# Weighing a head pair's values over eight query blocks instead of four, with row sums inverted once per half and the bias products opening the scores' sum

## The reference

```python
qkv = x @ w_qkv.T
qkv = qkv.reshape(b, t, dh, 3, h).transpose(3, 0, 4, 1, 2)
q, k, v = (qkv[0], qkv[1], qkv[2])
scores = jnp.einsum('bhid,bhjd->bhij', q, k) * scale
rel = jnp.arange(t)[None, :] - jnp.arange(t)[:, None] + (t - 1)
bias = rel_bias[rel]
scores = scores + bias.transpose(2, 0, 1)[None]
attn = jax.nn.softmax(scores, axis=-1)
out = jnp.einsum('bhij,bhjd->bhid', attn, v)
out = out.transpose(0, 2, 1, 3).reshape(b, t, h * dh)
return out @ w_out.T
```

## Time and profile before

| what | value |
|---|---|
| median of three runs | 2592.14 us |
| the profiled execution | 2590.8 us |
| its span, first to last instruction | 2589.0 us |
| PE busy over the span | 2448.0 us (95%) |
| DVE busy | 2157.6 us (83%) |
| ACT busy | 2032.1 us (78%) |
| POOL busy | 1519.4 us (59%) |
| PE matmuls of L1907 | 16384, 294.7 us busy |
| mean granted TensorE clock | 0.985 of full speed |

### The profile page before, as it was taken

How to read it: one execution, slowest core, us unless ns; L and a number is a source line. 1 busy time by engine, 2 the same in 40 slices (tenths; PEclk the granted TensorE clock), 3 DMA queues, 4 the chain that set the end, 5 groups by cost and what they waited for, 6 DMA issues and landing times. The chain is left out here.

```text
span 2589.0 us, 118567 instructions
## 1 busy us (share of the span) xinstructions
PE 2448.0 (95%) x52349; PEld 1956.1 (76%) x52349; DVE 2157.6 (83%) x2455; ACT 2032.1 (78%) x4077; POOL 1519.4 (59%) x1029
## 2 busy tenths in 40 slices
PE   6799999999999999999999998699999999997999
PEld 2478888888888888888888887367776777775787
DVE  5798888889888888888888886489888988895898
ACT  4689988989999898888999886667676766764776
POOL 3788888888888888887898874123222222222110
PEclk9999999999999999999999999799999999999999
DMA  3244434443444344434443332113132323221221
GB/s 96 52 98 95 109 78 96 95 110 84 99 100 98 84 93 98 96 87 97 104 99 83 85 82 60 46 43 74 40 71 49 67 47 67 50 60 28 83 74 41
DMA packets 275793, 202.01 MB, mean 78 GB/s; under 512 B 117568, under 2 KB 215880, under 8 KB 274248
## 3 DMA queue, kind: packets, MB, share of 16 engines
q1 hardware_dynamic: 275280, 194.42, 31.6%
HBM read 36.96 MB, written 1.11 MB: 15 GB/s over the span
## 5 line engine op out<-in xcount | busy, mean ns | idle before, releaser
L516 POOL TENSOR_TENSOR lt_t_sin<-lt_qk,lt_tab 128x512 f32<-128x512 f32 x384 | 685.5, 1806 | 218.9 <-DVE lt_qk L1302 216.8
L521 POOL TENSOR_TENSOR lt_qr<-lt_qr,lt_t_sin 128x1024 f32<-128x1024 f32 x192 | 455.5, 2373 | 28.1 <-POOL lt_t_sin L516 0.5
L2084 DVE TENSOR_REDUCE fa_neg_max<-bank 128x1 f32<-128x1024 f32 x256 | 301.5, 1219 | 94.1 <-PE bank L1881 92.4
L2006 ACT ACTIVATE fa_prob<-bank,fa_neg_max 128x1024 f32<-128x1024 f32 x128 | 142.6, 1114 | 217.9 <-DVE fa_neg_max L2084 165.5
L1907 PE MATMUL bank<-fa_prob_t,fa_v 32*64 32x128 f32 x16384 | 294.7, 277 | 19.2 <-issue 14.6
L1907 PEld LDWEIGHTS bank<-fa_prob_t,fa_v 32*64 32x64 f32 x16384 | 245.3, 131 | 80.6 <-issue 60.3
L2094 DVE STREAM_TRANSPOSE fa_prob_t<-fa_prob 128x1024 f32<-128x1024 f32 x256 | 302.1, 1218 | 0.0
L609 PE MATMUL bank<-lt_w_high,lt_x_high 128*128 128x512 f32 x576 | 262.4, 456 | 0.3 <-ACT lt_qk L981 0.3
L981 ACT COPY lt_qk<-bank 128x512 f32<-128x512 f32 x384 | 227.6, 594 | 30.6 <-POOL lt_t_sin L516 3.2
L1302 DVE TENSOR_TENSOR lt_qk<-lt_qk,lt_rn 128x2048 f32<-128x2048 f32 x96 | 242.0, 2520 | 2.6 <-ACT lt_rn L1007 2.6
L1295 DVE TENSOR_REDUCE lt_ssq<-lt_qr 128x32 f32<-128x2048 f32 x96 | 218.9, 2280 | 25.4 <-ACT lt_qr L989 25.4
(11 more groups left out here) (260 smaller groups left out, 5843.8 us busy)
## 6 DMA issues: line engine op xcount, KB each, us to landing
lt_v<-lt_v_tok SPq DMA_DIRECT2D x576, 128.0 KB
fa_v<-fa_v_tok SPq DMA_DIRECT2D x256, 128.0 KB, 2.7
lt_v<-lt_v_tok SPq DMA_DIRECT2D x192, 64.0 KB
lt_k_t<-lt_k_t SPq DMA_DIRECT2D x84, 128.0 KB, 3.0
lt_v<-lt_v SPq DMA_DIRECT2D x168, 64.0 KB, 2.1
lt_w_raw<-in_lt_wqkv_dram SPq DMA_DIRECT2D x36, 256.0 KB, 3.7
ex_cw_all<-cw_kept SPq DMA_DIRECT2D x8, 1024.0 KB, 4.6
lt_x_s<-h_in SPq DMA_DIRECT2D x96, 64.0 KB, 2.5
```

Of the source, the lines that this page charges most:

```text
L516: pool.tensor_tensor(dst[:, :, i, :], src[:, :, 1 - i, :], tab[:, g // 2 % 2, 1, at:at + 32].unsqueeze(1).to_broadcast([P, HEADS, 32]), AL ...
L521: pool.tensor_tensor(qr[:, g % 2, half], qr[:, g % 2, half], t_sin[:, :], ALU.add).then_inc(S.rotated, 1)
L2084: dve.tensor_reduce(neg_max[:, u % 2, par:par + 1], bank[:, 2 * par:2 * par + 2, :].rearrange("p a n -> p (a n)"), AX.X, ALU.max, negate=T ...
```

## The change

In the place of two quads per half there is one group of eight units:

- `weigh_v` weighs all eight units of a half, an eighth of the keys per step, over the eight steps of the next half: 32 matmuls per step with 256 moving columns. They are no longer cut in two.
- `prob_t` has one buffer of eight units of the same total size. It is filled alternately along one axis and along the other: unit j of a half writes where step j of the weighing has just read, so `turn` now waits in every step for that step's weighing (semaphore `av`).
- Banks 4 to 7 hold 256 columns of weighed values. ACT copies them out (128 x 1024) after the steps 2, 5 and 7 of a half (`LASTS`) into rows of `h_mid`; POOL adds the three partial sums (`add_att`) and multiplies once by the inverses (128 x 1024).
- The row sums of a half are inverted and turned once, in the fifth step (`u % QB == 4`); the inverses then go through DRAM and come back spread over partitions (`widen_inverse`, four DMAs out and two in per half). PE's spread, ACT's copy of it, and POOL's widening are gone.
- In near blocks the bias products come ahead of the scores, head by head: the first head's once the first head's exponents are done (`probs` 3(u-1)+1), the second head's one exponent later.
- Projections stand in steps 0, 2, 3, 4, 6 and 7, outputs in steps 1 and 5; `STEPS` is ten longer.

The core of the diff:

```diff
-        STEPS = range(UNITS + 2 * UPQ)
+        STEPS = range(UNITS + 2 * QB + 2)
...
+                    if qb >= 6:
+                        cols = slice(P, 2 * P) if qb == 6 else slice(0, 2 * P)
+                        for par in range(2):
+                            pe.wait_ge(S.probs, 3 * (u - 1) + 1 + par)
+                            for n, r in enumerate((rel_high, rel_low)):
+                                pe.matmul(bank[:, 2 * par, 0:P * (qb - 5)], anti[:, :], r[:, par, cols],
+                                          start=n == 0, stop=False, skip_group_check=True)
...
-                                mm = pe.matmul(bank[d, 4 + a, 0:P].rearrange("p (u r) -> p u r", u=UPQ),
-                                               v[rows, half % 2, kb, d],
-                                               prob_t[rows, q % 2, par, :, 32 * kb:32 * kb + 32],
-                                               start=kb == 0, stop=kb == KB - 1, skip_group_check=True)
+                                p = prob_t[rows, par, t, :, cols] if half % 2 else prob_t[rows, par, :, t, cols]
+                                mm = pe.matmul(bank[d, 4 + a, 0:JW].rearrange("p (u r) -> p u r", u=QB),
+                                               v[rows, half % 2, kb, d], p, start=i == 0 and t - 1 in (-1,) + LASTS,
+                                               stop=i == KBS - 1 and t in LASTS, skip_group_check=True)
...
                     if u + 1 < UNITS:
                         scores(u + 1)
                     wait_emptied(pe, u - 1)
...
+                    if half is not None:
+                        weigh_v(half, u % QB)
+                    for n in outs_at(u):
                         project_out(n, fresh)
-                    for j in jobs:
+                    for j in jobs_at(u):
                         job(j, fresh)
...
+                def empty_att(half, part):
+                    if half >= 1 and part < 2:
+                        act.wait_ge(S.att_t, half)
+                    if part == 2:
+                        act.wait_ge(S.att_sum, 2 * half + 1)
+                    act.copy(att(min(part, 1)), bank[:, 4:8, 0:JW]).then_inc(S.att, 1)
...
                 def turn(u):
-                    q = u // UPQ
-                    if u % UPQ == 0 and q >= 2:
-                        dve.wait_ge(S.av, UPQ * (q - 1))
+                    half, j = u // QB, u % QB
+                    if half >= 1:
+                        dve.wait_ge(S.av, QB * (half - 1) + j + 1)
                     for par in range(2):
                         dve.wait_ge(S.probs, 3 * u + 1 + 2 * par)
-                        dve.transpose(prob_t[:, q % 2, par, u % UPQ, :], prob[:, u % 2, par, :]).then_inc(S.turned, 1)
+                        if half % 2:
+                            dve.transpose(prob_t[:, par, :, j, :], prob[:, u % 2, par, :].rearrange("p (g n) -> p g n", g=QB))\
+                               .then_inc(S.turned, 1)
+                        else:
+                            dve.transpose(prob_t[:, par, j, :, :].rearrange("p g n -> p (g n)"), prob[:, u % 2, par, :])\
+                               .then_inc(S.turned, 1)
...
+                    if u % QB == 4 and weighed_at(u) is not None:
+                        invert(weighed_at(u))
+                        turn_inverse(weighed_at(u))
...
+                def add_att(half, n):
+                    pool.wait_ge(S.att, 3 * half + n + 1)
+                    if n == 2:
+                        pool.wait_ge(S.att_sum, 2 * half + 1)
+                    pool.tensor_tensor(att(0), att(0), att(1), ALU.add).then_inc(S.att_sum, 1)
...
+                def widen_inverse(half):
+                    sp.wait_ge(S.inv_t, half + 1)
+                    if half >= 1:
+                        sp.wait_ge(S.inv_in, 32 * half)
+                    for a in range(4):
+                        sp.dma_start(inv_kept[:, 32 * a:32 * a + 32], inv_t[32 * a:32 * a + 2 * QB, :]).then_inc(S.inv_kept, 16)
+                    sp.wait_ge(S.inv_kept, 64 * (half + 1))
+                    if half >= 1:
+                        sp.wait_ge(S.att_t, half)
+                    for par in range(2):
+                        kept = inv_kept[QB * par:QB * par + QB, :].rearrange("(o u) q -> o (u q)", o=1)
+                        sp.dma_start(inv_all[HD * par:HD * par + HD, :], kept.to_broadcast([HD, N])).then_inc(S.inv_in, 16)
```

More of the change, by code:

```diff
@@ L1829, in _ @@
                 for u in STEPS:
[L1830 to L1836 removed]
+                    for n in outs_at(u):
+                        add(n)
                     for j in jobs_at(u):
```

247 lines of the change are left out of this document (95 added, 152 removed).

## The result

| what | before | after |
|---|---|---|
| median of the runs | 2592.89 us (4 runs, 2589.5 to 2596.79) | 2566.10 us (4 runs, 2562.47 to 2567.15) |
| the profiled execution | 2590.8 us | 2562.47 us |
| its span | 2589.0 us | 2560.7 us |

The ratio is 0.9897, with a 95% interval of 0.9881 to 0.9913: faster by 1.0%, 26.8 us between the medians where 17 was forecast. The time lies inside the range, 9 us under the forecast.

A forecast was written before the change was run, and what follows sets the result against it. Per plain step, the loop (4.93 us), PE (4.71) and DVE (4.64) were taken as near-equal limits. 2590.8 + 2.5 (start) - 32 (steady halves) + 14.2 (end) = 2575 us, range 2562 to 2602.

The forecast's parts named there:

- Three limits close together: In a plain step the loop (4.93 us), PE (4.71) and DVE (4.64) lie within 0.3 us of each other.
- The steps cut in two: Three steps that made 15.5 of 20.40 us, and the last (5.38), become like the plain one, 4.93 us, once uncut.
- The weighing itself: PE's group of 64 wide passes per step still takes 2.10 us, since the columns account for the whole.
- The copies: ACT's 128 x 1024 copy takes 1.08 us; PE waits 0.57; next step 5.28 twice per half, 5.06 after the sixth.
- Bias products first: Near blocks: first head's pair leaves the path, second head's costs about 0.40 us; steps take 5.33 and 5.38 us.
- The inversion: Fifth step: about 0.5 us on DVE ahead of a near step's maximum, 5.14 against 5.33, hidden.
- Sum per half: Eight steps take 41.1 us instead of 42.52; with stalls 41.5 instead of 43.66, -32 us over 14.875 halves.
- The stalls: PE standing still, mostly in its weighing: 1.14 us per half falls to 0.4, bounds 0 and 1.1.
- Start: First eight units, without weighing on PE for eight instead of four, mostly at half clock: +2.5 us.
- End: From the last unit's first maximum to the next stage: 43.3 us instead of 29.1, +14.2 us.
- the gain was not eaten: Rival: weighing, turning and copy are coupled, so stalls stay at 1.14 us: 2586, or 2595 with a longer copy; 13%.
- The rival of passes costing by their number: Halving the passes gives back up to 0.2 us per group, steps behind copies 5.1, end 2 shorter: 2566 us; 9%.

The follow-up runs named there:

- e5: The changed kernel with 8 more matmuls (16 passes of 256 columns) at the end of each weighing group but the last half's: 2588.17 us, ratio 0.9977.
- e4: The kernel before with its weighing uncut in the second and third step of each quad, projections behind it: 2596.44 us, ratio 1.0006.
- e1b: The changed kernel with 128 weighing passes of 128 columns per step, two in a row per tile as in the kernel before: 2613.18 us, ratio 1.0061.
- e2: The changed kernel with the bias products back between the two parts of the scores: 2584.13 us, ratio 0.9959.
- e3: The kernel before with only the bias products moved ahead of the scores, head by head: 2589.21 us, ratio 0.9978.
- e7: The changed kernel with four more matmuls per step, results never read, in the first eight steps to keep PE busy: 2558.51 us, ratio 0.9863.

## Why the prediction was right, and what was mis-sized

**Three limits close together.** Right. Steps that the loop sets take 4.92 to 4.94 us (forecast 4.93), and e5 shows which steps are PE's: the same load costs them 0.4 us and the others 0.05.

**The steps cut in two.** Right for a clean half: e4 takes 0.9 us off it by uncutting alone. But the time did not follow there, and the prediction did not see that it could not.

**The weighing itself.** Forecast 2.10 us, measured 1.98. The columns set the pace, and e1b, with the old number of passes, is back at 2.10: 64 passes fewer give back 0.12 us. The Trainium skill ("TensorEngine Tiling (Array Packing)", Instruction Overhead) counts about 60 cycles per matmul, worth 0.2 us here by the prediction's estimate; measured is a little over half of that. In the plain steps it is worth nothing, since the loop sets them.

**DVE's wait for the weighing.** Right: 2.8 us over 564.

**The copies.** 1.05 us instead of 1.08, the wait of PE 0.51 instead of 0.57, the step behind it 5.14 and 5.11 instead of 5.28, since group and projections take 1.92 and 1.06 us on the path instead of 2.03 and 1.1. After the sixth step 5.01 instead of 5.06.

**Bias products first.** Right: 5.29 and 5.35 against 5.33 and 5.38, and e2 gives the part its own price, 14.4 us.

**The inversion.** Hidden, but with nothing to spare. It takes DVE 0.66 us (2096.96 to 2097.62), not 0.5, so that DVE is free for the maximum at 2097.62, when PE's scores, begun at 2095.98 and 1.69 us long, are ready at 2097.67. The margin of 5.14 against 5.33 was not there; cheaper bias products would have gained next to nothing in this step.

**Sum per half.** 40.79 instead of 41.1, 4.6 us over the stretch. This came from the group and the copies, not from new mechanisms. DVE's work on the bias table was left out of the sum, and costs 0.04 us per pair.

**The stalls.** This term was mis-sized: put at 0.4 us per half with bounds of 0 and 1.1, it measured 0. Its 0.4 x 14.875 = 6 us are the largest single miss, and the way of counting was wrong too. The prediction took the stalls as an addition to the steps. By the runs they come up where PE gets through a packet's 256 instructions before the next are there: shortening the steps in the kernel before made more of them (9.7 us became 12.5 in e3 and 21.4 in e4), and giving the changed kernel its old count of instructions brought them back (e1b). Counted so, the gain of 41.8 us splits into two parts: steps of 40.79 us instead of 42.52 (1.73 x 14.875 = 25.7, of which the bias products are 14.4 and the rest, 11.3, the uncut steps and the missing spread), and an intake that lets them run at that length (16.1). The second part also holds a stretch at half clock behind one of the stalls before (0.50 from 1822.4 to 1825.6). The shorter steps without the smaller intake gave 3.1 us (e3) and a loss of 2.3 (e4); the smaller intake with the old steps is in no run. The reason given, half the instructions to take in for the weighing, holds, and that it is the intake itself the 62 waits show, each of which ended at the first instructions of a packet, 1.2 to 1.6 us behind its landing. The Trainium skill ("Runtime: NRT & Kernel Launch", Instruction fetch mechanics) states that crossing from one block of instructions to the next is mostly hidden. The trace does not agree for this kernel: 21.4 us of such waits in e4, up to 2.4 us each.

**Start.** Forecast +2.5 us, measured -0.3. The clock was below full over the start, as expected. That the sum came out as before is chance: the first step took 6.9 us where 8.5 had stood, and both lengths occur in the profiles of the changed kernel's variants, whatever the edit. The other seven took 1.3 us more, the last four of them, for which the 2.5 was forecast, 23.9 us instead of 23.2. The 48 us depend on which steps get the full clock: over the profiles of this study without e7's edit, M(0) to M(8) lies between 46.7 and 50.7 us.

**End.** 45.0 us against 43.3. The weighing took 31.4 instead of 29.4. The start at + 7.1, the groups at full clock (1.8 us each) and the waits for copies (1.17 and 2.05 us for 3.0) are about as forecast; the 1.5 us for stalls are the term that fails, since there was none, but two stretches at half clock, which the sum did not have, cost 1.3 and 1.7 us (5.03 and 5.40 against 3.71). The rest took 13.7 against 13.9.

**The rivals.** Wide passes overlap as well as narrow ones, and the gain was not eaten, though e1b shows that its coupling exists: a stall there reaches DVE. The rival of passes costing by their number came about in part. It named the mechanism of the 0.12 us and the steps of 5.1 us behind copies, and its 2566 is the time that was measured. But its reason is not what made that time: the group's share of the gain is at most 0.31 us per half, 4.6 us, half of the 9 us between forecast and median; the end got longer where it had it shorter. That the figures meet is luck.

## What to carry to other kernels

Before you price the shortening of a step, look for the waits of TensorE that nothing releases, in the midst of a run of short matmuls, and at how often the instruction queue must deliver: if there are such waits, see whether they end a fixed time behind an instruction packet (here 1.2 to 1.6 us). Where they do, shorter steps alone can come back as more stalls, and the first thing to cut is the number of instructions. An edit's price can then differ by kernel; test it alone in both, and look for waits of its own, as e3's for POOL. At the end of a stage, look at the granted clock before you call a slow group a stall. Where a stage starts with little on TensorE, look at the granted clock, and consider filling the gap.

## What was not expected of the hardware

Four passes in a row on one tile of the array, with eight tiles in turn, make 128 passes of 128 columns take 2.82 us; with two in a row they take 2.10.

PE stood still at the border of two instruction packets, for up to 3.6 us, in all five kernels with 128 passes in a weighing group, and in the steady part of none with 64.

One edit's gain depended on the rest of the kernel: bias products first gave 14.4 us in the changed kernel and 3.1 in the kernel before, where a wait for POOL and more stalls took the rest.

DVE did an addition of 128 x 1024 in 1.23 us that took POOL 1.99, and POOL's multiplication with permuted blocks took 2.32 where its addition takes 1.99.
